# A five-part edit of a fused four-layer kernel: where layer 1's weight sums are taken, and in which order four phases begin

## What is computed

```python
x = x + _L0_xattn_ref(_layernorm(x), ctx, ...)   # 1 head of 256
x = x + _L0_ffn_ref(_layernorm(x), ...)          # top 2 of 8, two silu experts
x = x + _L1_xattn_ref(_layernorm(x), ctx, ...)   # 8 heads of 128
x = x + _L1_ffn_ref(_layernorm(x), ...)          # ternary weights, activations rounded
x = x + _L2_xattn_ref(_layernorm(x), ctx, ...)   # 16 heads of 64
x = x + _L2_ffn_ref(_layernorm(x), ...)          # 8 experts, linear
x = x + _L3_xattn_ref(_layernorm(x), ctx, ...)   # 16 heads of 64
x = x + _L3_ffn_ref(_layernorm(x), ...)          # 8 experts with silu, and a shared one
```

```python
def _weight_quant(w):
    scale = 1.0 / jnp.clip(jnp.mean(jnp.abs(w)), 1e-05)
    wq = jnp.clip(jnp.round(w * scale), -1.0, 1.0) / scale
    return w + jax.lax.stop_gradient(wq - w)

def _act_quant(x):
    scale = 127.0 / jnp.clip(jnp.max(jnp.abs(x), axis=-1, keepdims=True), 1e-05)
    xq = jnp.clip(jnp.round(x * scale), -128.0, 127.0) / scale
    return x + jax.lax.stop_gradient(xq - x)
```

## Time and profile before

| | |
|---|---|
| median of 3 runs | 1838.39 us (1838.14 to 1839.67) |
| the profiled execution | 1833.6 us, span 1831.8 us |
| mean granted clock of TensorE | 0.986 |
| PE / DVE / ACT / POOL busy | 1727.3 / 1390.8 / 1037.4 / 636.6 us |
| the same as shares of the span | 94 / 76 / 57 / 35% |
| layer 0's FFN starts, ends on DVE | 105.89, 135.03 |
| layer 1's FFN starts | 945.71 |
| attentions of layers 2 and 3 start | 1005.17, 1410.70 |

### The profile page before, as it was taken

How to read it: one execution, slowest core, us unless ns; L and a number is a source line. 1 busy time by engine, 2 the same in 40 slices (tenths; PEclk the granted TensorE clock), 3 DMA queues, 4 the chain that set the end, 5 groups by cost and what they waited for, 6 DMA issues and landing times. The chain is left out here.

```text
span 1831.8 us, 31026 instructions
## 1 busy us (share of the span) xinstructions
PE 1727.3 (94%) x11308; PEld 1528.6 (83%) x11311; DVE 1390.8 (76%) x3101; ACT 1037.4 (57%) x2291; POOL 636.6 (35%) x904
## 2 busy tenths in 40 slices
PE   6979999999999999999978899999979999999799
PEld 6657898999989998989875788888857888888698
DVE  6568787877778787878767677777777788888775
ACT  3355656555655655554655566666650677777542
POOL 0613030210203030302100465656661467666542
PEclk9999999999999999999999999999989999999899
DMA  5011000000000000000020111111000000000111
GB/s 177 34 54 38 1 24 1 1 24 1 24 1 24 1 24 1 16 1 1 1 92 7 67 62 55 61 56 61 10 1 18 9 16 17 17 10 4 31 54 42
DMA packets 19480, 52.19 MB, mean 28 GB/s; under 512 B 2809, under 2 KB 7554, under 8 KB 17666
## 3 DMA queue, kind: packets, MB, share of 16 engines
q1 hardware_dynamic: 18466, 49.39, 8.1%
q10 hardware_dynamic: 864, 0.83, 0.1%
HBM read 49.29 MB, written 0.92 MB: 27 GB/s over the span
## 5 line engine op out<-in xcount | busy, mean ns | idle before, releaser
L1476 ACT ACTIVATE a_pH<-banks 125x512 fp32r<-125x512 f32 (+1 forms) x384 | 203.5, 544 | 268.3 <-PE banks L221 193.8
L1573 DVE TENSOR_TENSOR a_pL<-banks,a_pH 125x512 fp32r<-125x512 f32 (+1 forms) x384 | 235.9, 623 | 107.1 <-ACT a_pH L1476 105.1
L2160 POOL TENSOR_TENSOR a_prob<-a_prob,a_rinv 112x750 f32<-112x750 f32 x128 | 184.0, 1437 | 190.2 <-DVE a_rinv L2484 189.7
L1537 DVE TENSOR_SCALAR_CACHE_REDUCE a_prob<-banks 128x500 f32<-128x500 f32 x336 | 221.5, 677 | 4.8 <-PE banks L221 3.9
L1312 POOL TENSOR_TENSOR a_head_oH<-a_o,ones 128x256 fp32r<-128x256 f32 (+1 forms) x23 | 15.6, 678 | 579.5 <-DVE a_o L1581 579.5
L1358 PE MATMUL banks<-ident,a_prob 128*125 128x128 f32 x1344 | 201.3, 274 | 4.5 <-ACT a_prob L1455 2.3
L1455 ACT ACTIVATE a_prob<-a_prob,a_nmax 128x1000 f32<-128x1000 f32 x168 | 187.9, 1121 | 30.7 <-DVE a_nmax L1540 30.7
L221 PE MATMUL banks<-a_pH,a_head_vH 125*128 125x256 f32 (+1 forms) x576 | 199.8, 347 | 5.2 <-DVE a_pL L1573 4.2
L1358 PEld LDWEIGHTS banks<-ident,a_prob 128*125 128x125 f32 x1344 | 186.3, 188 | 7.5 <-DVE a_head_qL L1171 3.5
L221 PE MATMUL banks<-a_pH,a_head_vL 125*128 125x256 f32 (+1 forms) x576 | 173.2, 301 | 0.0
L221 PE MATMUL banks<-a_pL,a_head_vH 125*128 125x256 f32 (+1 forms) x576 | 172.4, 299 | 0.0
(11 more groups left out here) (401 smaller groups left out, 4870.6 us busy)
## 6 DMA issues: line engine op xcount, KB each, us to landing
a_w_out<-in_f_out SPq DMA_DIRECT2D x6, 1024.0 KB, 4.8
a_w_in<-in_f_in SPq DMA_DIRECT2D x12, 512.0 KB, 4.7
f_raw<-in_f_w SPq DMA_DIRECT2D x9, 513.0 KB, 3.6
pair_raw<-in_a_qk SPq DMA_DIRECT2D x16, 256.0 KB, 2.6
pair_raw<-in_a_w SPq DMA_DIRECT2D x8, 384.0 KB, 3.0
combined<-in_f_w SPq DMA_DIRECT2D x12, 256.0 KB, 3.0
a_v<-in_ctx_rows SPq DMA_DIRECT2D x4, 576.0 KB, 7.5
a_kT<-in_f_w SPq DMA_DIRECT2D x2, 1024.0 KB, 5.7
```

Source lines behind the costliest of these rows:

```text
L1476: act.activation(pH[:, c % RING, 0:wide], TB[c % 4][0:KB, 0:wide], ACT.Copy).then_inc(t_high, 1)
L1537: dve.tensor_scalar(prob[:, at, c * CHUNK:(c + 1) * CHUNK], SB[c % 3][:, 0:CHUNK], SCALE, None, ALU.mult, ALU.max, accum_out=chunk_max[:, ...
L1573: dve.tensor_tensor(pL[:, c % RING, 0:wide], TB[c % 4][0:KB, 0:wide], pH[:, c % RING, 0:wide].bitcast(F32), ALU.subtract).then_inc(t_done, 1)
L2160: pool.tensor_tensor(both, both, rinv[:, n % RING, :].unsqueeze(2).to_broadcast([SEQ, 2, KEYS]), ALU.mult).then_inc(p_normed, 1)
```

## The change

1. The three sums leave `layer0_attention`, with their transfers, the product and the scaled copy.
2. They come into `layer0_ffn`. It has a buffer of its own for the three pieces, which are loaded at the phase's start behind router weights, expert weights and bias. ACT takes the Abs in place (SBUF to SBUF) behind the silus of tiles 0, 1 and 2. PE adds the sums up between tiles 5 and 6, in the router's bank. Two chunks of keys instead of three are made ahead, and four behind tiles 2 to 5.
3. In `layer1_ffn` ACT loads the silu table first, then takes the high halves of three chunks of keys, the seven scalings, and the other three chunks. Before it was five chunks, the table, the scalings, one chunk.
4. In both attentions of 16 heads the second half of the queries is made behind scores 1, instead of in the first step, and PE makes all values that are left (`LAST_VALUES`) behind scores 2: three in layer 2, five in layer 3. Before, values were spread between scores 0, 1 and 2.
5. In layer 2 DVE takes the low halves of two values (`EARLY`) before those of x.

```diff
@@ -228,7 +228,6 @@
...
     TURN_AT, QUERIES_AT = 8, 10
-    QUANT = 2048
     SCORES_AT = KTILES // 2 - 1
@@ -267,10 +266,6 @@
...
         tail_high = spare[:, NK:NK + NK // PIECES].bitcast(F32R)
-        flat_kT = kT[:].rearrange("p e n -> p (e n)")
-        quant_raw = [flat_kT[:, 0:QUANT], flat_kT[:, QUANT:2 * QUANT], raw_tail[:, 0:QUANT]]
-        abs_out = s.psum[:, 0:QUANT]
-        abs_sum = sb("a0_abs_sum", [P, 3])
         oT = xT
@@ -303,9 +298,6 @@
...
         head_loaded, head_high, head_cut = sem("a0_head_loaded"), sem("a0_head_high"), sem("a0_head_cut")
...
         qn = next_norm_semaphores(sem, "a0")
@@ -332,11 +324,6 @@
...
             sp.dma_start(s.pair.head_raw, dram["a1_w"][0]).then_inc(head_loaded, 16)
-            sp.wait_ge(s_filled, BATCH)
-            for m in range(3):
-                if m == 2:
-                    sp.wait_ge(cut_done, 3 * PIECES)
-                sp.dma_start(quant_raw[m], dram["f1_w"][:, m, :]).then_inc(quant_loaded[m], 16)
 
@@ -519,13 +506,6 @@
...
                     exps(b + AHEAD)
-            act.wait_ge(t_done, BATCH)
-            for m in range(3):
-                act.wait_ge(quant_loaded[m], 16)
-                need(act, abs_summed, m)
-                act.activation(abs_out, quant_raw[m], ACT.Abs, accum_out=abs_sum[:, m:m + 1]).then_inc(abs_summed, 1)
-            act.wait_ge(abs_total, 1)
-            act.activation(s.w_mean[:], B[4][:, 0:3], ACT.Copy, scale=1.0 / (P * QUANT)).then_inc(mean_ready, 1)
             load_table(act, s, ACT.Sqrt, n=2)
@@ -638,8 +618,6 @@
...
                 output_tile(i)
-            pe.wait_ge(abs_summed, 3)
-            pe.matmul(B[4][:, 0:3], s.ones[:], abs_sum[:], start=True, stop=True).then_inc(abs_total, 1)
 
@@ -777,8 +755,14 @@
...
         POST = 4
-        KEYS_AHEAD = 3
-        KEYS_BEHIND = (3, 4, 5)
+        KEYS_AHEAD = 2
+        KEYS_BEHIND = (2, 3, 4, 5)
+        QUANT = 2048
+        SUMS = 3
+        quant_raw = sb("f0_quant_raw", [P, SUMS, QUANT])
+        abs_sum = sb("f0_abs_sum", [P, SUMS])
+        quant_loaded = [sem(f"f0_quant_loaded{m}") for m in range(SUMS)]
+        abs_summed, abs_total, mean_ready = sem("f0_abs_summed"), sem("f0_abs_total"), sem("f0_mean_ready")
         xn = sb("f0_xn", [P, TILES, D])
@@ -812,6 +796,8 @@
...
             sp.dma_start(bias[:], dram["f0_bias"]).then_inc(bias_loaded, 16)
+            for m in range(SUMS):
+                sp.dma_start(quant_raw[:, m, :], dram["f1_w"][:, m, :]).then_inc(quant_loaded[m], 16)
 
@@ -878,8 +864,13 @@
...
                 act.activation(post[:, i % POST, :], EB[i % 4][:, :], ACT.Silu).then_inc(post_ready, 1)
+                if i < SUMS:
+                    act.wait_ge(quant_loaded[i], 16)
+                    act.activation(quant_raw[:, i, :], quant_raw[:, i, :], ACT.Abs, accum_out=abs_sum[:, i:i + 1]).then_inc(abs_summed, 1)
                 if i in KEYS_BEHIND:
                     key_high(KEYS_AHEAD + KEYS_BEHIND.index(i))
+            act.wait_ge(abs_total, 1)
+            act.activation(s.w_mean[:], B[3][:, 0:SUMS], ACT.Copy, scale=1.0 / (P * QUANT)).then_inc(mean_ready, 1)
             load_table(act, s, ACT.Sqrt, n=2)
@@ -910,6 +901,10 @@
...
                     keys(KEYS_AHEAD + KEYS_BEHIND.index(i))
+                if i == TILES - 2:
+                    pe.wait_ge(abs_summed, SUMS)
+                    pe.wait_ge(q.shifted, 1)
+                    pe.matmul(B[3][:, 0:SUMS], s.ones[:], abs_sum[:], start=True, stop=True).then_inc(abs_total, 1)
 
@@ -1653,6 +1648,7 @@
...
     COMBINED_AT = {1: 0, 3: 1, 5: 2, 6: 3}
+    KEYS_FIRST = 3
     with ExitStack() as ctx:
@@ -1797,13 +1793,14 @@
...
             layer_norm_scalar(act, ln, ql)
-            for c in range(CHUNKS - 1):
+            load_table(act, s, ACT.Silu)
+            for c in range(KEYS_FIRST):
                 key_high(c)
-            load_table(act, s, ACT.Silu)
             act.wait_ge(x_step, 4)
...
                 act.activation(big[:, i, :], xn[:, i, :], ACT.Copy, scale=scale[:, i:i + 1], bias=MAGIC).then_inc(x_scaled, 1)
-            key_high(CHUNKS - 1)
+            for c in range(KEYS_FIRST, CHUNKS):
+                key_high(c)
             for g in range(GROUPS):
@@ -1968,7 +1965,7 @@
...
     def queries_at(h, b):
-        return [(0, 1)] * (h == 0 and b == 0) + [(h + 1, n) for n, at in enumerate(QUERIES_AT) if at == b and h + 1 < HEADS]
+        return [(h + 1, n) for n, at in enumerate(QUERIES_AT) if at == b and h + 1 < HEADS]
 
@@ -2005,10 +2002,15 @@
...
         count("v", (0, u))
+    NEXT = AHEAD_VALUES
+    LAST_VALUES = [u for u in range(NEXT + 4, UNITS) if u not in FIRST_VALUES_AT]
     count("q", (0, 0))
-    for u in range(AHEAD_VALUES, UNITS):
-        if u not in FIRST_VALUES_AT:
-            count("v", (0, u))
+    for u in range(NEXT, NEXT + 3):
+        count("v", (0, u))
+    count("q", (0, 1))
+    count("v", (0, NEXT + 3))
+    for u in LAST_VALUES:
+        count("v", (0, u))
     for h in range(HEADS):
@@ -2341,18 +2343,17 @@
...
             queries(0, 0)
-            values(0, AHEAD_VALUES)
+            values(0, NEXT)
             pe.wait_ge(ql.done, GROUPS)
             scores(0, 0)
-            for u in range(AHEAD_VALUES + 1, 5):
+            for u in (NEXT + 1, NEXT + 2):
                 values(0, u)
             scores(0, 1)
-            values(0, 5)
+            queries(0, 1)
             turn(0)
-            for u in (6, 7):
-                values(0, u)
+            values(0, NEXT + 3)
             scores(0, 2)
-            for u in (8, 9):
+            for u in LAST_VALUES:
                 values(0, u)
@@ -2521,26 +2521,27 @@
...
                 keys(0, c)
+            EARLY = max(VALUES_BEFORE - 1, 0)
+            for u in range(EARLY):
+                values(0, u)
             turn_vector(dve, ql, LNB, s.xnTH, s.xnTL)
...
                 keys(0, c)
-            for u in range(AHEAD_VALUES):
+            for u in range(EARLY, AHEAD_VALUES):
                 values(0, u)
             queries(0, 0)
-            values(0, AHEAD_VALUES)
+            values(0, NEXT)
             maxima(0)
-            for u in range(AHEAD_VALUES + 1, 4):
+            one_over_sums(0)
+            for u in (NEXT + 1, NEXT + 2):
                 values(0, u)
-            one_over_sums(0)
-            values(0, 4)
             maxima(1)
-            values(0, 5)
+            one_over_sums(1)
+            queries(0, 1)
             turned(0)
-            one_over_sums(1)
-            for u in (6, 7):
-                values(0, u)
+            values(0, NEXT + 3)
             maxima(2)
-            for u in (8, 9):
+            for u in LAST_VALUES:
                 values(0, u)
```

More of the change, by code:

```diff
@@ L305, in layer0_attention @@
         head_loaded, head_high, head_cut = sem("a0_head_loaded"), sem("a0_head_high"), sem("a0_head_cut")
-        quant_loaded = [sem(f"a0_quant_loaded{m}") for m in range(3)]
-        abs_summed, abs_total = sem("a0_abs_summed"), sem("a0_abs_total")
-        mean_ready = sem("a0_mean_ready")
         qn = next_norm_semaphores(sem, "a0")
```

## The result

The kernel got faster: median 1829.88 us (1827.85 to 1831.9, 6 runs) against 1838.54 (1837.86 to 1840.28, 6 runs) of the kernel before on the same chip. The ratio is 0.995, with a 95% interval of 0.9938 to 0.9963. The saving was forecast as 5.6 us and is 8.7. But the two profiled executions differ by only 2.8: before took 1833.6 us at a mean granted clock of 0.986, the changed kernel 1830.8 at 0.983 (span 1829.0). The difference between these two comparisons is the subject of most that follows.

What follows compares the result with a forecast made beforehand. TensorE, busy 94% of the span, was taken as the bound, so edits pay only where it waits at phase starts and ends. -2.05 + 1.06 - 2.0 - 3.5 + 0.85 = -5.6 gave 1832.8 us, range 1829.8 to 1836.2.

Steps and rivals of the forecast that it cites:

- A: Layer 0's attention: with the sums gone DVE ends the phase, and the next starts at 103.84, 2.05 us earlier.
- B: Layer 0's FFN: taking in the sums makes four tiles carry a low half instead of three, +1.06 us (-0.6 to +1.6).
- C: Layer 1's FFN: table and scalings earlier bring ACT's copies of turned activations forward, -2.0 us (bounds 1.0 and 3.0).
- D: Layer 2's start: earlier queries and shorter queues from exps to exps bring scores 4 forward, -3.5 us (-2.6 to -4.4).
- my first rival, The other clock rival: Clock falls at new places, in layer 2's first products and two FFN starts: saving 3.3, 1835.1 us; chance 0.18.
- E: Layer 3's start: five values before scores 3 wait for DVE to empty a bank, +0.85 us (-0.8 to +2.05).
- the last one of the sum: Whole kernel: the profiled saving of 5.6 us carried over to the median, 1838.4 to 1832.8.
- the clock stays up where it was down: Shorter waits at four starts keep TensorE's clock up, saving 2.0 us more: 1830.8 us; chance 0.13.

Runs made afterwards that it cites:

- second profile of the changed kernel: The changed kernel run once more with nothing altered, beside the two kernels that fill layer 2's 2.28 us wait: median 1829.7 us, ratio 0.9953 to the kernel before.
- the idle products: Ten repeated products of the last unit of values added in layer 2's first step, against the changed kernel: median 1826.6 us beside 1829.7.

## Why the prediction was right or wrong

- **A, right.** -2.05 forecast, -2.2 measured; the gap was 1.15 instead of 1.30.
- **B, right in mechanism, 0.3 too dear.** I took 1.92 for a sum with its reading; from silu to silu 2.39 passed instead of 2.47. The in-place sum at 1.91 confirms that SBUF as destination costs next to nothing beside the 1.88 into PSUM. The Trainium skill ("ScalarE: Activation LUTs", "Step-by-step: what each stage is for") calls PSUM the faster destination; the trace agrees in direction, by 0.03. The pieces were never late.
- **C, the length right, the clock missed.** I forecast the copies 2.0 earlier. Behind the phase's first product the copies came after 12.7 before and 10.7 now, 2.0 earlier. But the phase became 3.35 shorter, and 4.0 us went from the median. The rest is the slow stretch behind the copies. I had it in the bounds (3.0) for another reason.
- **D, the chain right, what came behind it missed.** Exps 1 to 3 were within 0.07 of my sums. Counted from the phase's start, scores 4 came at 27.1, 2.2 earlier than the 29.25 of before, not 3.5: in the profiled execution the slow stretch of the first products lay at the very start of the phase, where I had full clock. In the second profile of the changed kernel, which had 1.00 there, they came at 25.67, 3.6 earlier. Where I wrote that TensorE "is idle for about 1 us still", I had looked only at the first product. Moving queries out of the first step left 2.28 us before scores 4, and the clock fell just there. That is my first rival, in a place I had not named; the idle products price it at 3.1 us. Still the layer's start was worth more than 3.5 by the medians, 5.9 alone, since the old order lost clock as well, behind its wait on queries: layer 2's attention took 354.3 to 355.2 in five of the six profiles with the old order, and 350.9 only in the one that I built on; with the new order and its wait it took 350.5 to 352.5.
- **E, right.** Scores 4 stand 17.36 behind exps 0; forecast 17.38, before 16.54: +0.82 for the forecast +0.85. PE's wait for DVE's low half is there (1.22). The phase itself is 0.85 shorter in the pair above, but over all profiles it took 308.4 to 311.2 with the old order and 310.3 to 311.9 with the new as it stands. By the runs the new order costs about 1.9 at equal clock. In the profile of the changed kernel there is again a slow stretch behind the waits of 1.22 and 1.45, but not in its second profile; where the rest of the 1.9 comes from stays open.
- **The step that failed** is the last one of the sum: "The median of the runs is 4.8 higher, and the same saving gives 1832.8." The 4.8 was no fixed cost around the span but clock: the profiled execution had 0.986 and its typical sisters 0.981. A change that alters idle times alters how often that loss occurs, so it can't be carried over. At equal clock the saving was 6.2 for my 5.6; another 0.002 to 0.003 of clock brought it to 8.7. That the lengths came out so near is in part luck: layer 2's start was worth 1.2 more than I took and layer 3's cost 1.1 more. The rival "the clock stays up where it was down" was the one that came true on balance, at 1830.8, and I gave it 0.13. The other clock rival showed itself in the profile at the same time.

## What to carry to other kernels

When the profiled execution differs from the median by more than the runs differ among themselves, look at the clocks of the runs first, and price the change at equal clock; then ask for each changed wait of TensorE whether it gets longer or shorter, because in layer 2 that is where the rest came from. Add up the queues of the engines that wait for each other, as here from exps to exps: such sums were right to a few hundredths of a microsecond. And when an item is taken out of a queue, look what now stands empty at its old place; the cheapest mend is to put other useful work there.

## What the runs showed of the hardware

I had not expected that 0.006 in the mean clock is 6 us in runs of one and the same kernel (mean times of 1840.1 at 0.980, 1833.6 at 0.986), nor that a wait of 2.28 us of TensorE in the middle of dense work is followed by ten microseconds at 0.50, four times the wait itself, while waits of 1.1 in the same place were followed by none. Adding ten products that compute nothing new made the kernel 3.1 us faster. In layer 1's FFN the same remedy at a wait of 1.92 did not work, a wait of 1.72 there was followed by no slow stretch, and in layer 2's old order waits of 1.48 and 0.98 mostly were. So the length of a single wait isn't all that decides; what else does is open.
